# Second sequence's expert outputs weighted on ScalarE and summed on GpSimd, two splits of maxima on GpSimd, an MLP output in tiles, and a new order table

## The reference, cut to what matters

```python
# layer 0: x (2, 512, 128)
nx = layer_norm(x); evidence = softmax(nx Wq (proto Wk)^T / sqrt(128)) (proto Wv)
combined = concat([nx, evidence, anchor])
router_probs = softmax(combined @ router_W + router_b)
h = silu(einsum('btc,ecr->bter', combined, e_w1) + e_b1)
expert_out = einsum('bter,erh->bteh', h, e_w2) + e_b2
routed = sum(expert_out * router_probs[..., None], axis=-2)
g = sigmoid(silu(combined @ gate_w1 + gate_b1) @ gate_w2 + gate_b2)
x = x + g * (routed @ out_w + out_b)
# layer 1
h = layer_norm(x) * (1 + scale_msa) + shift_msa
x = x + (mha(h Wq, h Wk, h Wv) @ self_o_w + self_o_b) * gate_msa
h = layer_norm(x) * norm2_g + norm2_b
x = x + mha(h q_w, context kv_k, context kv_v) @ cross_o_w + cross_o_b
h = layer_norm(x) * (1 + scale_mlp) + shift_mlp
x = x + (gelu(h @ mlp_w1 + b1) @ mlp_w2 + b2) * gate_mlp
```

## Time and profile before

| | us |
|---|---|
| median of 3 runs | 274.73 (274.42 to 274.83) |
| the profiled execution | 274.17 |
| its span, first to last instruction | 272.30 |
| TensorE busy | 240.0 |
| VectorE busy | 171.0 |
| ScalarE busy | 149.7 |
| GpSimd busy | 46.1 |

### The profile page before, as it was taken

The page is one execution under the profiler, slowest core; times in us unless marked ns, Lnnn a source line. Parts: engine busy times, 40 slices in busy tenths (PEclk is TensorE's granted clock), DMA queues, the critical chain, the costliest instruction groups (busy, mean ns, idle before and its releaser), DMA issues.

```text
span 272.3 us, 4953 instructions
## 1 busy us (share of the span) xinstructions
PE 240.0 (88%) x1832; PEld 134.6 (49%) x1851; DVE 171.0 (63%) x393; ACT 149.7 (55%) x277; POOL 46.1 (17%) x60
## 2 busy tenths in 40 slices
PE   7699999797778899999999889999899896978966
PEld 3366686356424333343435444554445454446655
DVE  6955328343999999676997965896523335228141
ACT  1225213744005658675767577857975763585552
POOL 1403710049314600000200020001030001201120
PEclk9999999999979999999999999999999997599999
DMA  6999991034440003552030002100002100030001
GB/s 183 402 172 178 164 159 19 2 95 124 131 116 24 15 19 87 161 147 67 13 102 23 5 4 60 30 2 6 2 0 70 42 1 5 4 82 4 19 6 35
DMA packets 19117, 18.93 MB, mean 70 GB/s; under 512 B 3613, under 2 KB 17133, under 8 KB 18677
## 3 DMA queue, kind: packets, MB, share of 16 engines
q1 hardware_dynamic: 18957, 18.54, 28.1%
q10 hardware_dynamic: 136, 0.07, 0.1%
HBM read 13.83 MB, written 2.24 MB: 59 GB/s over the span
## 4 chain that ended last, share of the span: by engine, by line
PE 56%; DVE 23%; ACT 10%; issue 6%; DMA 4%; SPq 1%; POOL 0%; DVEq 0%; ACTq 0%; POOLq 0%
PE ps L1211 52%; DVE neg_max L1085 10%; ACT region L808 6%; DVE neg_max L1094 2%; DMA Qs<-q_scr 2%; DVE normed L910 1%; PE ps L1507 1%; ACT pv_sb L817 1%; PE ps L1248 1%; DVE stats L894 1%; DMA x_sb<-in_x 1%; DVE routed L1042 1%; DMA q_scr<-q_parts 1%; DVE max_parts L1111 1%; PE ps L1440 1%
## 5 line engine op out<-in xcount | busy, mean ns | idle before, releaser
L808 ACT ACTIVATE region<-ps 128x512 f32<-128x512 f32 (+1 forms) x160 | 86.7, 594 | 34.2 <-PE ps L1211 32.8
L1085 DVE TENSOR_REDUCE neg_max<-ps 128x2 f32<-128x1024 f32 x64 | 75.8, 1218 | 12.6 <-PE ps L1211 11.6
L1211 PE MATMUL ps<-Qs,k_room 128*128 128x256 bf16 x256 | 42.0, 275 | 2.4 <-ACT region L808 0.5
L1211 PE MATMUL ps<-k_room,Qs 128*128 128x512 bf16 x113 | 34.5, 383 | 8.9 <-DVE neg_max L1085 5.5
L585 POOL TENSOR_TENSOR rstd<-var_eps,minus_half 128x2 f32<-128x2 f32 (+1 forms) x12 | 9.7, 811 | 178.7 <-DVE var_eps L899 178.7
L1211 PE MATMUL ps<-region,V 128*32 128x256 f32 x512 | 37.1, 388 | 0.4 <-ACT pv_sb L817 0.4
L1211 PEld LDWEIGHTS ps<-Qs,k_room 128*128 128x128 bf16 x256 | 19.7, 97 | 24.5 <-ACT region L808 15.3
L1211 PEld LDWEIGHTS ps<-k_room,Qs 128*128 128x128 bf16 x128 | 9.7, 98 | 21.4 <-DVE neg_max L1085 10.9
L1211 PEld LDWEIGHTS ps<-region,V 128*32 128x32 f32 x512 | 12.2, 108 | 14.9 <-issue 7.6
L1094 DVE TENSOR_REDUCE neg_max<-ps 128x8 f32<-128x616 f32 x16 | 12.2, 795 | 6.6 <-PE ps L1211 6.4
L797 ACT ACTIVATE max_rows<-ps 24x256 bf16<-24x256 bf16 (+2 forms) x14 | 5.2, 369 | 18.3 <-PE ps L1440 18.3
(11 more groups left out here) (165 smaller groups left out, 322.3 us busy)
## 6 DMA issues: line engine op xcount, KB each, us to landing
k_room<-k_scr SPq DMA_DIRECT2D x4, 576.0 KB
Qs<-q_scr SPq DMA_DIRECT2D x24, 96.0 KB
Qs<-q_parts SPq DMA_DIRECT2D x35, 64.0 KB
k_room<-in_pad SPq DMA_DIRECT2D x2, 896.0 KB
Qs<-in_pad SPq DMA_DIRECT2D x4, 448.0 KB
region<-in_w_hidden SPq DMA_DIRECT2D x1, 1344.0 KB, 7.7
w_attn<-in_w_attn SPq DMA_DIRECT2D x1, 896.0 KB, 10.9
k_scr<-k_parts SPq DMA_DIRECT2D x4, 192.0 KB, 2.9
```

The lines of the kernel that those rows point to most:

```text
L808: nc.scalar.activation(probs[0:rows_, s % UNITS, j0:j0 + CT // 2, :], ps[0:rows_, EXP0 + e % 2, :].rearrange("p (j n) -> p j n", n=TU), AC ...
L1085: nc.vector.tensor_reduce(neg_max[:, b, t, h:h + MH], ps[:, bank:bank + MH, :], axis=AX, op=ALU.max, negate=True).then_inc(max_read, 1)
L1211: return nc.tensor.matmul(out, lhsT, rhs, start=start, stop=stop)
```

## The change

Five things.

1. Second sequence's experts. ScalarE evicts each expert's 128x128 block from PSUM and scales it by the routing weight (`weigh_expert`, 12 operations), into a new area `weighted` carved out of `region`. GpSimd turns the gate from tanh to sigmoid and folds it and x into the bias (`gate_bias`, three operations on 128x512), then adds the three experts, multiplies by the gate and adds the bias, per pair of tiles (`blend_experts`, two times four operations on 128x256). VectorE's `expert_sum` and `gated_sum` remain for the first sequence. VectorE waits for `x1_ready` before the second sequence's first statistics, and so does ScalarE before it writes exponentials over that area.
2. The second and third `split_maxima` (the other half of group 0's heads and group 1 of unit 0) move from VectorE to GpSimd.
3. `FIRST_MAXIMA` is 2, not 4.
4. Unit 1's `mlp_down` is made tile by tile, as that of units 2 and 3 was, in banks EXP0 and EXP0+1 instead of MAX0; its output goes out in two stores.
5. The table is new. Above all, the first split, its transpose and the first exponentials stand some maxima earlier; the sequence-0 weight fold of GpSimd stands after `keys:0`; the last part has three more warm-up products.

```diff
-expert_bias:0 hidden_x:0.4 hidden_x:0.5 weights:2 hidden:0.4 scores_T:1 hidden:0.5 hidden_x:0.6 fold:0 hidden:0.6
+expert_bias:0 hidden_x:0.4 hidden_x:0.5 weights:2 hidden:0.4 scores_T:1 hidden:0.5 hidden_x:0.6 hidden:0.6
...
-hidden_x:1.1 hidden:1.1 hidden_x:1.2 apply:1.0 hidden:1.2 warm:5.3 norm_T:1.0 keys:0 queries:0 hidden_x:1.3
+hidden_x:1.1 hidden:1.1 hidden_x:1.2 apply:1.0 hidden:1.2 warm:0.3 norm_T:1.0 keys:0 fold:0 queries:0 hidden_x:1.3
...
+        weighted = carve(NEXP * T).rearrange("p (e t c) -> p e t c", e=NEXP, t=NT)
...
-        FIRST_MAXIMA = 4
+        FIRST_MAXIMA = 2
+        POOL_SPLITS = range(1, 3)
...
-            return t if u >= FINE else tuple(range(NTU))
+            return t if u else tuple(range(NTU))
...
-        DOWN_BANK = [(MISC,), (MAX0,), (MAX0 + 1, MAX0), (MISC, PVB)]
+        DOWN_BANK = [(MISC,), (EXP0, EXP0 + 1), (MAX0 + 1, MAX0), (MISC, PVB)]
...
+            def gate_bias(b):
+
+                pool.wait_ge(g2_tanh, b + 1)
+                pool.wait_ge(x1_in, 16)
+                own(nc.gpsimd.tensor_scalar(gate[:, :, :], gate[:, :, :], 0.5, 0.5, ALU.mult, ALU.add))
+                own(nc.gpsimd.tensor_tensor(x_bias[:, b, :, :], x_bias[:, b, :, :], gate[:, :, :], ALU.mult))
+                own(nc.gpsimd.tensor_tensor(x_bias[:, b, :, :], x_bias[:, b, :, :], x_sb[:, b, :, :], ALU.add))
+
+            def blend_experts(b, pair):
+
+                tiles = slice(2 * pair, 2 * pair + 2)
+                pool.wait_ge(e2_weighed, tiles.stop)
+                total = weighted[:, 0, tiles, :]
+                for e in range(1, NEXP):
+                    own(nc.gpsimd.tensor_tensor(total, total, weighted[:, e, tiles, :], ALU.add))
+                own(nc.gpsimd.tensor_tensor(total, total, gate[:, tiles, :], ALU.mult))
+                ins = nc.gpsimd.tensor_tensor(x_sb[:, b, tiles, :], total, x_bias[:, b, tiles, :], ALU.add)
...
             for stage, n in STAGES:
-                if stage == "expert_bias":
+                if stage == "max_split" and split_turn(*n) in POOL_SPLITS:
+                    split_maxima(*n)
+                elif stage == "expert_bias":
                     expert_bias(n)
+                elif stage == "shift":
+                    gate_bias(n)
+                elif stage == "blend":
+                    blend_experts(n, 0)
+                elif stage == "gated" and n == 1:
+                    blend_experts(n, 1)
...
+            def weigh_expert(b, t):
+
+                act.wait_ge(rt_ready, b + 1)
+                act.wait_ge(e2_raw, NT * b + t + 1)
+                for e in range(NEXP):
+                    ins = nc.scalar.activation(weighted[:, e, t, :], ps[:, OUT_BANK[b][t], e * C:(e + 1) * C],
+                                               ACT.Copy, scale=route[:, b, t, e:e + 1])
+                ins.then_inc(e2_weighed, 1)
...
+                if 3 <= s < UNITS:
+                    act.wait_ge(x1_ready, B)
...
             def norm_stats(k, n):
+
+                if (k, n) == (1, 1):
+                    dve.wait_ge(x1_ready, B)
...
-                elif stage == "expert":
+                elif stage == "expert" and n[0] == 0:
...
-                elif stage == "gated":
+                elif stage == "gated" and n == 0:
...
-                elif stage == "max_split":
+                elif stage == "max_split" and split_turn(*n) not in POOL_SPLITS:
...
-                read_by(bank, e2_read, NT * b + t + 1)
+                read_by(bank, *((e2_weighed, t + 1) if b else (e2_read, t + 1)))
```

136 lines of the change are left out of this document (79 added, 57 removed).

## The result

The changed kernel takes **279.24 us**, the median of 20 runs (274.28 to 283.82); the kernel before, run beside it, 274.65 (20 runs, 271.64 to 280.20). The ratio is 1.0121, 95% interval 1.0084 to 1.0157. The change is slower, and the median lies above the predicted range of 272.1 to 277.3. The ratio leaves disturbed runs out and the medians do not, so it is smaller than their quotient. The profiled execution took 276.06 us, 1.89 more than the one of before, so one pair of profiles shows less than half of the difference of the medians, 4.59.

The account below looks back on a forecast made before the run. VectorE was taken to set the pace from 66.4 to about 106 us, then TensorE. 274.17 - 1.75 + 0.8 + 0.1 + 1.1 = 274.4, on the median's scale 275.0 us; range 272.1 to 277.3.

Parts of the forecast that it names:

- The fold beside the normalization: First sequence's weight fold on GpSimd meets VectorE's four normalizations at 48 us: +0.1 us, bounds 0 and 1.1.
- First split held by the blends: VectorE's first split of maxima, at 73.75 us, has its casts wait for GpSimd's blends: +0.8 us, bounds 0 and 2.0.
- rival B: GpSimd holds VectorE longer, at first split's subtractions and the fold at 48 us: 276.2 to 277.2 us, chance 0.18.
- Three stalls: VectorE idles before maxima 9, 12 and 13, waiting for scores: 1.0, 1.1 and 1.1 us.
- Rival A: The stalls before maxima 9, 12 and 13 don't come: 2.5 of 3.3 us vanish, 272.5 us, chance 0.32.
- ScalarE's twelve evictions at 0.28, GpSimd's x ahead of VectorE: Second sequence: evictions take 3.4 us, covered; GpSimd's x at 75.9 us, VectorE needs it at 78.05.
- Marker 1.75 us earlier: Start of self maximum 24 on VectorE comes at 104.55 us instead of 106.31; bounds 5.0 earlier, 1.5 later.
- Rival C: VectorE's freed time becomes idling before scores, maximum 24 stays at 106.31 us: 276.7 us or less, chance 0.08.
- What is gained at the marker is kept: From maximum 24 on, TensorE's groups keep nearly the same order, so the gain stays, except for the last 40 us.
- Last 40 us: Warm-up products before the last query +0.4, around last cross maxima +0.35, MLP output's bank +0.35: +1.1 us, bounds 0 and 1.5.
- Cross groups reordered: Reordered cross groups between 150 and 225 us cost 0, TensorE having the same groups; bounds -0.5 and +0.5.
- The scale, +0.56: Step from the profiled execution, 274.17 us, to the median of the kernel before's three runs, 274.73: 0.56 us added.

Follow-up runs that it names:

- a_both_back: Changed kernel with the sequence-0 weight fold and the last part (table and banks) put back as before; 275.21 us, ratio 0.998 to the kernel before.
- a_splits_dve: a_both_back with the second and third split of maxima on VectorE again, the second right behind maximum 7; 276.25 us, ratio 1.004.
- a_best: a_rows plus eleven products of zeros on TensorE, and maxima 14, 15 and 16 placed earlier; three measurements, medians 268.92, 271.38 and 268.73 us.
- a_rows_warm: a_both_back plus the rows' transfer ahead of unit 1's key and query loads and eleven products of zeros, stalls not repaired; 270.62 us (4 runs).
- b_tail_moved: Kernel before with only the last part changed (three more warm-up products, unit 1's MLP output in two tiles on the exponentials' banks); 275.17 us, ratio 1.003.
- after_warm: Changed kernel plus eleven products of zeros where TensorE idled, nothing else moved; 275.49 us (12 runs), ratio 1.006 to the kernel before.
- b_fold_moved: Kernel before with only the first sequence's weight fold moved behind keys:0; 275.97 us, ratio 1.004.
- a_tail_back: Changed kernel with only the last part of the table and the banks put back as before; 275.77 us, ratio 1.002.
- a_stalls: a_both_back with the scores of maxima 9, 12 and 13 moved ahead in TensorE's order; 272.23 us (6 runs), ratio 0.990.
- a_rows: a_stalls with the fourth split's transposed maxima and their transfer ahead of unit 1's key and query loads; median 272.65 us (4 runs).

## Why the prediction was wrong

Two steps failed. Between the profiles the sum said +0.25 us and +1.89 was measured: the fold's term and the gain at the marker were wrong. From the profile to the median it said +0.56, taken from the kernel before, and 3.18 was measured; with 0.56 the median would have been 276.6, inside the range.

- *The fold beside the normalization, +0.1 (bounds 0 and 1.1)*: **this term failed**. The four normalizations took 1.80 us longer. Of that 0.26 was covered by ScalarE's earlier work and not 0.4 (ScalarE took up the transposes at 50.22 us, though the earlier trace rows show its earlier row ending at 50.34). So keys came 1.43 later, and maximum 0 1.96 later at the clock of that profile. I let two short GpSimd operations, or one long one, hold a normalization. In fact each of the four operations held one: VectorE's operation ends when GpSimd's ends, the next two begin within 0.1 us of each other, and VectorE loses again. The bound should have been the whole of GpSimd's queue that can lie beside a VectorE sequence, 2.85 us, less the sequence's own time.
- *First split held by the blends, +0.8*: right. The casts took 0.31 and 0.58 in place of 0.17, 0.55 us too long in sum, and 0.65 and 0.58 in a_both_back, 0.89 too long. That the subtractions stayed at 0.17 is no evidence against rival B. Each began 0.01 to 0.02 us ahead of GpSimd's next operation, in the gap that the held cast had ended in. Where one began inside an operation (a_splits_dve) it took 0.40.
- *Three stalls, 1.0 + 1.1 + 1.1*: right in place and size, 0.77 + 1.27 + 1.27. Rival A, in which they do not come, fell.
- *ScalarE's twelve evictions at 0.28, GpSimd's x ahead of VectorE*: right. The evictions take 0.30 each; x was ready at 78.5 us and VectorE got there at 80.54. It was half a us past the 78 that I had named as the limit, because GpSimd's work on the gate began at 68.72 us and not at 65.45; with fold and last part undone x was ready at 75.25, where I had put 75.9. The third split also had its cover: it was done at 99.42, and TensorE came to its transpose at 101.05 without a wait.
- *Marker 1.75 us earlier*: **wrong**. It is 1.26 later, and with fold and last part undone 0.36 earlier. Of that gap of 1.4 the hold on the split is 0.9, which I had added apart; the rest is matched by the idle time ahead of maximum 24 itself, 0.63 us, which I had not counted.
- *Rival C, the freed time turns into idling*: near to what happened. VectorE's idle time ahead of the self maxima grew from 12.6 to 18.2 us, and without fold and last part the change gains 0.36 us at the marker and nothing in the runs. Its condition, that TensorE is the limit up to the marker, did not hold: with the order of TensorE's work changed (a_best against a_rows_warm), 1.5 us were won.
- *"What is gained at the marker is kept"*: wrong. Between maxima 24 and 32 the changed kernel lost 0.63 us, of which 0.59 is TensorE's wait for the rows' transfer. Counting groups in TensorE's order did not show that TensorE comes to this group earlier than its transfer, which stands behind 576 KB.
- *Last 40 us, +1.1*: right, 1.08 in the profiles and 0.93 at full clock, but with luck in the pieces: the bank was taken too small (0.6, not 0.35) and the products too large (about 0.35, not 0.75).
- *Cross groups reordered, 0 (bounds -0.5 and +0.5)*: at the edge. From maximum 32 to the addition a_both_back takes 107.77 us and b_tail_moved, with the table of before there, 108.23, both at full clock: 0.5 us won.
- *The scale, +0.56*: **this step failed** too. I set the sum against one execution of the kernel before and moved it by 0.56 us, the distance of three runs. The changed kernel's median lies 3.18 us above its profiled execution. With a clock of 0.981 that execution was among the better ones of its kernel, whose median is 0.975. The low stretch near 227 to 237 us, which I had named as a sign, shrank from 10.3 to 6.8 us, and a new one came at 53.3. The fold and the last part go with a lower clock (median 0.975 with both, 0.981 with either undone), though the kernel before has 0.975 with neither. The medians say 279.24 with both, 275.79 and 275.77 with either undone, and 275.21 with neither: not a sum. That the second costs little in the median once the first is gone is measured; that the clock has a large share is supported by after_warm, whose median is 3.75 us lower with no wait taken away. Why these two parts together bring the clock down is not shown.
- *Rival B* was right in sign and in its second half, that the fold's long operation holds a normalization; it was the third, and the short ones held the other three. Its first half, held subtractions, did not come in this kernel. Its 276.2 to 277.2 still lie below the median.

The Trainium skill's page "SBUF — State Buffer", section "SBUF: two separate sides", says that the loser of the shared ports is fully blocked; the rows agree (2.92 us). It also says that the one that starts first has them for the whole instruction. By the rows of the changed kernel a normalization that begins 0.07 us ahead of GpSimd's operation still ends 0.09 after it, while the subtractions of 0.17 us that begin 0.01 to 0.02 ahead are not held; the order of recorded starts does not tell who wins.

What stays open: why a low stretch comes in one execution and not in the next, how much of the 1.3 us that go with the clock belongs to each part, and how the 3.0 us at equal clock divide: the profiles account for about 1.4 to 2.0 (fold) and 0.9 (last part).

## What to carry to other kernels

Moving work from VectorE to GpSimd also moves the rest of GpSimd's queue: look at what will newly lie beside casts and normalizations of VectorE, and price it at the whole of GpSimd's queue there, not at one operation (here 1.8 us, not 0.1). Time freed on the engine that sets the pace is worth something only if the next input is already there, so repair in the same edit what stands ahead of it, on TensorE and in the DMA queue. And compare runs at the same granted clock before you believe a difference under 2%; then ask separately what the change does to the clock.

## What the runs showed of the hardware that I had not expected

- A sequence of short VectorE operations beside a sequence of GpSimd operations takes GpSimd's time, one for one: 0.52, 0.61, 1.42 and 0.61 us for normalizations of 0.34, beside operations of 0.45, 0.45, 1.26 and 0.46, which are not slowed. In four kernels (changed, b_fold_moved, a_tail_back, after_warm) the sum was 2.92 or 2.93 us. The rows of this tile, changed kernel (durations in ns: least, median, greatest; first and last start):

```profile
L975 DVE TENSOR_SCALAR normed<-x_sb,mean_var,rstd x4: 519/610/1419, 48.0 to 50.3; 128x128 f32<-128x128 f32 x4
```
- The clock's low stretches differ between executions of one kernel, near 11, 52, 78 to 89 and 227 to 239 us, and the changed kernel's runs go from 274.3 us at 0.994 to 283.8 at 0.945, 1.9 us for 0.01 of the mean. Eleven products of zeros (2.4 us of TensorE's time at full clock, put where it idled) took 1.4 to 3.75 us off the median.
- A 12 KB transfer issued 3.6 us behind a 576 KB one let TensorE go on only 4.8 us after its issue (a_stalls); issued ahead of it and earlier, nobody waited (a_rows).
